# A hybrid decoder kernel on one core: the gated-delta stage goes from units of four heads by 512 tokens to units of eight heads by 256 tokens

## What is computed

```python
q, k, v = silu(causal_conv4(x @ Wq)), silu(causal_conv4(x @ Wk)), silu(causal_conv4(x @ Wv))   # per channel, 4 taps
g = -exp(A_log) * softplus(x @ Wfa @ Wfb + dt_bias);  beta = sigmoid(x @ Wb)
q = l2norm(q) * K**-0.5;  k = l2norm(k)
def step(S, qt, kt, vt, gt, bt):              # S: 128 x 128 per head, one step per token
    S = S * exp(gt)[..., None]
    vd = (vt - einsum('hkv,hk->hv', S, kt)) * bt[..., None]
    S = S + kt[..., None] * vd[:, None, :]
    return S, einsum('hkv,hk->hv', S, qt)
o = o * rsqrt(mean(o*o) + EPS) * o_norm_w * sigmoid(x @ Wga @ Wgb)
out = o @ Wo
```

## Time and profile before

| what | value |
|---|---|
| median of 3 runs | 3720.73 us |
| the profiled execution | 3717.97 us, span 3715.8 us |
| PE busy | 3474.6 us (94%), 37416 instructions |
| DVE, ACT, POOL busy | 1941.4, 1427.4, 125.0 us |
| mean granted TensorE clock | 0.965 |
| delta stage | about 912 to 3020 us of the span |

### The profile page before, as it was taken

The page is one execution under the profiler, slowest core; times in us unless marked ns, Lnnn a source line. Parts: engine busy times, 40 slices in busy tenths (PEclk is TensorE's granted clock), DMA queues, the critical chain, the costliest instruction groups (busy, mean ns, idle before and its releaser), DMA issues. The chain is left out here.

```text
span 3715.8 us, 86134 instructions
## 1 busy us (share of the span) xinstructions
PE 3474.6 (94%) x37416; PEld 1694.5 (46%) x37416; DVE 1941.4 (52%) x3334; ACT 1427.4 (38%) x3313; POOL 125.0 (3%) x457
## 2 busy tenths in 40 slices
PE   6979999996789999999999999999999759999999
PEld 4454444442344544444444444444444435444444
DVE  2131111113778897789878878887888431111111
ACT  1010000001466656666665666566656521000000
POOL 0000000000000000000000000000000000000000
PEclk9979999997989999999999999999999868999999
DMA  4011100003111111121111111111211042000000
GB/s 154 7 57 36 28 0 29 11 0 120 48 31 36 42 50 34 45 66 41 33 56 43 48 50 45 42 37 39 65 39 34 16 154 63 14 15 29 0 12 12
DMA packets 83725, 156.21 MB, mean 42 GB/s; under 512 B 8782, under 2 KB 33998, under 8 KB 79516
## 3 DMA queue, kind: packets, MB, share of 16 engines
q1 hardware_dynamic: 83356, 150.77, 12.3%
HBM read 133.71 MB, written 17.04 MB: 41 GB/s over the span
## 5 line engine op out<-in xcount | busy, mean ns | idle before, releaser
L1333 PE MATMUL psum<-dl_xt,dl_wqkv 128*128 128x512 f32 x1536 | 778.2, 624 | 10.4 <-DVE dl_qkv L977 10.0
L513 DVE SCALAR_TENSOR_TENSOR f_act_g<-psum,f_bup,f_act_g 128x512 f32<-128x512 f32 x96 | 72.1, 751 | 939.4 <-ACT f_act_g L468 939.4
L977 DVE SCALAR_TENSOR_TENSOR dl_qkv<-psum,dl_par,dl_qkv 128x511 f32<-128x511 f32 (+2 forms) x576 | 430.4, 747 | 14.0
L468 ACT ACTIVATE f_act_g<-psum,f_bgate 128x512 f32<-128x512 f32 x96 | 66.0, 687 | 923.1 <-PE psum L411 923.1
L1333 PEld LDWEIGHTS psum<-dl_xt,dl_wqkv 128*128 128x128 f32 x1536 | 257.4, 189 | 250.2 <-issue 212.5
L411 PE MATMUL psum<-xnt_sb,wup 128*128 128x512 f32 x768 | 345.2, 592 | 0.0
L407 PE MATMUL psum<-xnt_sb,wgate 128*128 128x512 f32 x768 | 345.2, 592 | 0.0
L429 PE MATMUL psum<-f_wdown,f_hidden 128*128 128x512 f32 x768 | 344.9, 592 | 0.0
L1340 PE MATMUL psum<-dl_wo,dl_sg 128*128 128x512 f32 x512 | 260.9, 623 | 2.9 <-DVE dl_qkv L977 2.5
L407 PEld LDWEIGHTS psum<-xnt_sb,wgate 128*128 128x128 f32 x768 | 145.9, 190 | 183.7 <-issue 183.7
L411 PEld LDWEIGHTS psum<-xnt_sb,wup 128*128 128x128 f32 x768 | 145.9, 190 | 183.7 <-issue 183.7
(11 more groups left out here) (192 smaller groups left out, 4618.1 us busy)
## 6 DMA issues: line engine op xcount, KB each, us to landing
dl_wqkv<-in_dw_qkv SPq DMA_DIRECT2D x192, 256.0 KB, 2.6
dl_wo<-in_dwo SPq DMA_DIRECT2D x16, 1024.0 KB, 5.2
f_weights_b<-f_weights_by_expert SPq DMA_DIRECT2D x48, 256.0 KB, 6.3
wgate<-in_wgate SPq DMA_DIRECT2D x2, 3072.0 KB, 18.6
wup<-in_wup SPq DMA_DIRECT2D x2, 3072.0 KB, 24.7
f_wdown<-in_wdown SPq DMA_DIRECT2D x2, 3072.0 KB, 13.6
x_sb<-in_x SPq DMA_DIRECT2D x4, 1024.0 KB, 9.3
x_after_experts<-x_sb SPq DMA_DIRECT2D x16, 256.0 KB, 2.0
```

The costliest lines, as they stand in the source:

```text
L977: tap_ = lambda dl: dve.scalar_tensor_tensor(y_[:, dl:TT], ps[:, bank, 0:TT - dl], par[:, h, 4 * a + 3 - dl:4 * a + 4 - dl], y_[:, dl:TT], ...
L1333: last = pe.matmul(ps[:, bank, :], wq[:, n % RING, m, :], xt[:, u // HG % 2, m, :], start=(m == 0), stop=(m == KC - 1))
```

## The change

HU = 8 heads in a unit (two halves HE of HJ = 4), TT = 256 tokens, so again 16 units (2 head groups by 8 token tiles), of 8 slots. The scan's groups hold both halves: 16 instructions each. There are 24 "proj" jobs a unit, each four matmuls 128x259: the tile is loaded with the three tokens before it (HALO), so `boundary`, the tails and L984 go. "rows" is two 128-token tiles a unit, each summed over eight heads in one bank (in four parts q of two matmuls). Long jobs are whole, four a slot: one behind `output_inner`, two behind `solve_u` and the shorts at "inner", one behind `state_step`. All jobs share banks 4 to 7. `krow` and `vrow` use true transposes. GpSimd takes over the series, `near_zero`, `decayed`, the early keys and `o_scale`; level jobs are no longer halved. `choose` and `softplus` are one step behind `add_state` of slot 1. A silu waits for eight convolutions, of 256 tokens; the convolutions of a slot's first two or three long jobs now stand ahead of its `add_state`. The ring for weights is six, `wo` comes in quarters of 512 KB (64 loads), and the output tile is stored every second unit. Cut to its core:

```diff
-HG = 4
+HE = 2
+HU = HJ * HE
+HG = H // HU
-TT = 512
+TT = 256
-RING = 4
+RING = 6
+JOB_BANKS = (4, 5, 6, 7)
...
+def main_jobs(k, sl):
+    if sl in (3, 4):
+        jobs = [("rows", k - 1, i, q) for q in (2 * sl - 6, 2 * sl - 5) for i in range(RB)]
+    else:
+        unit, first = {0: (k + 1, 8), 1: (k + 1, 12), 2: (k + 1, 16), 5: (k + 1, 20), 6: (k + 2, 0), 7: (k + 2, 4)}[sl]
+        jobs = [("proj", unit, first + n, 0) for n in range(4)]
...
+    table = {(0, "long"): [("vrow", k, 1)], (0, "inner"): [("vrow", k, 2)], (0, "split"): [("vrow", k, 3)],
+             (1, "inner"): [("gate", p, 0), ("gate", p, 1)], (1, "split"): [("gate", p, 2)], (1, "end"): [("gate", p, 3)],
+             (2, "inner"): [("turn", p, 0), ("turn", p, 1)], (2, "split"): [("turn", p, 2)], (2, "end"): [("turn", p, 3)],
+             (3, "states"): [("level", w, 0)], (3, "long"): [("level", w, 1)], (3, "end"): [("level", w, 2)],
+             (4, "states"): [("sums", w, 0)], (4, "long"): [("level", w, 3)], (4, "end"): [("level", w, 4)],
+             (5, "long"): [("level", w, 5)],
+             (6, "long"): [("krow", w, 0), ("dec", w2, 0)], (6, "inner"): [("krow", w, 1), ("dec", w2, 1)],
+             (6, "split"): [("dec", w2, 2)], (6, "end"): [("dec", w2, 3)],
+             (7, "states"): [("cross", w, 0)], (7, "long"): [("krow", w, 2)], (7, "inner"): [("krow", w, 3), ("corner", w, 0)],
+             (7, "end"): [("vrow", w, 0)]}
```

GpSimd's order of work for each k, and the series (six operations on 128x2048):

```diff
+                    if prep:
+                        near_zero(w)
+                    if post:
+                        o_scale(p)
+                    if prep:
+                        decayed(w, QQ)
+                        decayed(w, KK)
+                        for lv in range(1, LEVELS + 1):
+                            early_keys(w, lv)
+                        solve(w)
+                    if ahead:
+                        series(w2)
...
+                    for n, c in enumerate((1.0 / 3.0, -0.5, 1.0)):
+                        if n == 0:
+                            pool.tensor_scalar(poly[:, :], all_w, -0.25, c, ALU.mult, ALU.add).then_inc(s["series"], 1)
...
+                        pool.tensor_tensor(poly[:, :], poly[:, :], all_w, ALU.mult).then_inc(s["series"], 1)
```

VectorE in a slot, `by_rows` on TensorE, and TensorE's order in a slot:

```diff
+                        convolutions(done_before, sl)
+                        if sl in (3, 4, 5) and prep:
+                            late_tokens(w, 2 * sl - 5)
                         if run:
                             add_state(k, sl)
...
+                        convolutions(done_behind, sl)
...
-                    for m in range(4):
-                        for j in range(HJ):
-                            last = pe.matmul(ps[part(j), bank, P * m:P * m + P], chunk(src, g0 + m)[:, j, :], ident,
-                                             start=True, stop=True)
+                        last = pe.transpose(ps[:, bank, P * m:P * m + P], src[:, g].rearrange("p j t -> p (j t)"), ident)
...
                         if put_out:
                             output_inner(*previous)
+                        all_main(main[0:1])
                         all_short(k, sl, "long")
                         if run:
                             solve_u(k, sl)
                         all_short(k, sl, "inner")
+                        all_main(main[1:3])
                         if run:
                             state_step(k, sl)
                         all_short(k, sl, "split")
+                        all_main(main[3:4])
                         all_short(k, sl, "end")
```

More of the change, by code:

```diff
@@ L544, in short_jobs @@
 def short_jobs(k, sl, at):
     w, w2, p = k + 1, k + 2, k - 1
[L548 to L562, removed]
@@ L564, in short_jobs @@
+    once = {(1, "end"): ("beta", w, 0), (3, "split"): ("ga", w, 0), (4, "split"): ("fa", w2, 0)}.get((sl, at))
     jobs = [once] if once and once[1] % HG == 0 else []
[L565 to L568, removed]
+    return [j for j in jobs + table.get((sl, at), []) if 0 <= j[1] < UNITS]
 def place_jobs():
-    used, place = [0] * 8, {}
@@ L589, in place_jobs @@
+    last = {job: n for n, job in enumerate(order)}
+    ends, used, place = {b: -1 for b in JOB_BANKS}, {b: 0 for b in JOB_BANKS}, {}
+    for job in order:
+        if job not in place:
+            bank = min(JOB_BANKS, key=lambda b: ends[b])
+            place[job] = (bank, used[bank])
+            used[bank] += 1
+            ends[bank] = last[job]
     return place
@@ L878, in inverse_norms, with shorts, taps @@
                     act.activation(f, f, ACT.Exp, scale=-0.5).then_inc(s["roots"], 1)
+                def shorts(k, sl, at):
+                    for job in short_jobs(k, sl, at):
+                        if job[0] not in ("level", "turn", "sums", "cross", "corner"):
+                            short(job)
+                def taps(jobs):
+                    for job, _ in jobs:
+                        if job[0] == "proj":
+                            tap(*job[1:])
                 for k in range(-2, UNITS + 1):
@@ L942, in _ @@
-                        if job and job[0] == "proj":
-                            tap(*job[1:])
-                        for job, _ in short_jobs(k, sl, "end"):
-                            if job[0] not in ("level", "turn", "sums", "cross", "corner"):
-                                short(job)
-                        if sl == 9 and prep:
-                            inverse_norms(w)
             @block.vector
@@ L1346, in by_rows @@
+                        if q == 3:
+                            last.then_inc(full[bank], 1)
+                        elif i == RB - 1:
+                            last.then_inc(s["wo_read"], 1)
+                def by_rows(bank, src, n):
                     for m in range(4):
[L1347 to L1349 removed]
```

843 lines of the change are left out of this document (407 added, 436 removed).

## The result

The changed kernel takes **4024.4 us** (median of four runs, 4014.1 to 4031.5) against 3720.6 us: 1.082 times as long, 95% interval 1.079 to 1.0845. The forecast was 3640 us, with 3555 to 3730 as its range: the sign is wrong, and the range misses by 294 us. The profiled execution of the changed kernel took 4025.6 us, with a span of 4023.8.

A forecast was written before the change was run, and what follows sets the result against it. TensorE's own instruction sequence was taken as the bound. A unit of 111.0 work plus 8.5 idle is 119.5 us, -70 over 15 steps; with -10 at the ends, 3718.0 becomes 3638, median 3640 us, range 3555 to 3730.

The forecast's parts named there:

- signs of being wrong: Wrong if projections start over 0.24 us apart, POOL takes over 5.5 us, or PE idles over 13 us a unit.
- the ends: Start and end of the kernel: -3 us at the start, -7 from about three slot pairs, -10 in all.
- PE's sum: TensorE's work per unit: scan groups -3.1, `krow` and `vrow` -4.6, edges -2.6, halo +0.8; 111.0 us needed.
- that rival (3790): Short projections pay for their weights, +10 us a unit with idle as forecast: 3790 us, chance 0.02.
- Transfers hidden: Weight loads, `wo` pieces and output stores stay hidden; if not, up to 2 us a unit.
- Where PE will wait: TensorE's idle time per unit, walked slot by slot: waits sum to 11.5 us, taken as 8.5, bounds 3.8 and 13.
- the taps behind the silus: ScalarE's taps stand behind silus: part of waits of about 2 us each in slots 0 and 6.
- banks held by convolutions one slot late: Rival: small waits, such as banks 4 to 7 held, eat the gain; idle 12 to 13, about 3715 us, chance 0.12.
- successive waits share their slack: An engine late in one slot is not later in the next for the same reason: 11.5 us becomes 8.5.
- GpSimd: Operations of 2048 elements at 3.9 us (upper end 7.7), early keys about 2; some 55 us of the unit's 115.
- POOL late: Rival: at 7.7 us an operation, `decayed` ahead of level 1 (slot 3) and `choose` (slot 1) delay: 3850 us, chance 0.15.
- The rival on the slower side: Slower outcome, chance 0.17: late GpSimd results (0.15, 3850 us) plus short projections paying for weights (0.02).

The follow-up runs named there:

- e14: Changed kernel with both `gated` of slot 2 on VectorE moved behind convolution 15, ahead of `add_state`: 3952.6 us, 1.062 times the kernel before.
- e15: Changed kernel with convolution 14 moved ahead of `choose` in slot 1 on VectorE: 3973.9 us, 1.067 times the kernel before.
- e1: Changed kernel with GpSimd's new operations cut to a sixteenth of their width, a probe that leaves out work: 3890.7 us, 1.046 times the kernel before.
- e7: Changed kernel with VectorE's three moves, the series' adds written with two operations, and ScalarE's later taps ahead of silus of q and v: 3803.0 us.
- e9: Changed kernel with GpSimd's new operations at 1/16 width (work left out), VectorE's three moves, and ScalarE's later taps ahead of silus of q and v: 3741.8 us.

## Why the prediction was wrong

Of the prediction's own signs of being wrong one came true: PE idles over 13 us a unit. By its own steps, for the profiled execution (4025.6 against 3638 forecast, 388 us): the unit came out 24.9 us too long (374 us), the ends -13.9 + 19.2 = +5 instead of -10.

- **PE's sum, 111.0 us: right.** 110 at the full clock. Projections start 0.23 us apart (2111.66 to 2113.51 us, eight), 0.01 above what 259 columns cost at 0.84 ns. So a short projection pays for its weights at most that, some 2 us a unit and not 10; that rival (3790) is out. The state step took 0.65 (2110.04 to 2110.69), not 0.86, which gives 1.7 of it back. Four full-width transposes at 2140.31 have the next group 0.53 behind them, as in the earlier trace rows.
- **Transfers hidden: right.** The loads take 2.6 and 3.6 us, and no wait for them stands among PE's costliest.
- **Where PE will wait, 8.5 us, bounds 3.8 to 13: the step that failed.** It is 26.2. The walk followed each engine's order only as far as the scan's own chain and the levels. It found the taps behind the silus (slots 0 and 6; mended, they are worth 31 to 47 us) and the tap behind the decay's Exps (slot 2), but not the two costliest waits, turn 2 on turn 0's bank and the next user of projection 14's bank (gate 3 or projection 16), 122 us by e14 and e15. It had no term either for the gaps without a releaser, 6.0 of the 26.2. The diff says that all jobs share banks 4 to 7; the prediction put "banks held by convolutions one slot late" into a rival of 12 to 13 us idle and 3715 us, without asking for each job which one held its bank before and where that one's reader stands. Also "successive waits share their slack", by which 11.5 became 8.5, is not borne out: taken away together, the causes give back their sum to within 14 us.
- **GpSimd: too small in price, and in the wrong place.** 3.9 us was taken for each of the 2048-element operations; they measure 4.5 for two tensors and 5.4 to 5.5 for the three of one operation, and only those come near the 5.5 of the rival "POOL late". The early keys take 3.38 us in the mean, not 2: 2.0 to 2.9 by themselves, and 4.1 to 5.0 where a VectorE product began before them. Its forecast place (`decayed` ahead of level 1, slot 3) is not where it hurts in steady work: from 1200 to 3100 us no row has PE waiting for L791. Before that, where the first units are prepared, PE waits 14.3 us for `decayed` and the early keys. The rest of its 134 us shows as VectorE's instructions stretched under it and as waits for the comparison. What GpSimd does to VectorE beside it was costed at nothing: VectorE's own times were taken as if GpSimd were idle, as in the earlier trace rows. VectorE is busy 92.6 us a unit, where about 85 was forecast, and 83.8 in e1. The Trainium skill (GPSIMD Engine Reference, 1) says that GpSimd contends with VectorE's instructions that have two SBUF inputs; the trace agrees, 3.72 against 1.26 us for L1099's 1024 elements with and without it. It also shows convolutions and `add_state`, with one input in PSUM, untouched (482 ns in both).
- **The clock: no term.** The sum priced all of PE's work at the full clock of the earlier trace rows. With the idle time the granted clock fell to 0.93 in the window, and 118.2 us of busy time took the place of 110: some 8 us a unit, about 120 us of the 388. With idle 15.5 us (e7) it is 0.96, with 13.6 (e9) 0.97.
- **The rival on the slower side** had GpSimd as its mechanism. That is a third (134 of 384 us); VectorE's and ScalarE's order around the shared banks are 147 to 163, and about 100 stay.

Of the 384 us between forecast and measurement e9 gives back 283 with three edits, one of which leaves work out. The rest is 13.6 instead of 8.5 idle, and 113.2 instead of 111.0 busy, a unit: (5.1 + 2.2) x 15 = 110. The 13.6 are 6.1 of gaps without a releaser and 7.5 of small waits ("level" and "cross" for VectorE, r, dec 0) that were left as they are. So the gaps alone exceed the 5.1 us by which the idle time is over the forecast; their cause stays open.

## What to carry to other kernels

When jobs share a rotation of PSUM banks, list for each job the one that held its bank before and the place of that one's last reader in its engine's queue; a wait there is as real as one in the recurrence, and TensorE pays it twice, in idle time and in clock. Work moved to GpSimd isn't free because GpSimd has room: price each form of operation by itself, and price what VectorE does in that time again. Then test a part at a time: of this change the u product behind a long job pays in the new order and true transposes of v pay in the old one, and the latter alone beats both kernels. And look at the idle time that has no releaser before you promise to remove the rest.

## What was not expected of the hardware

- A GpSimd `tensor_scalar` over 128x2048 float32 takes 5.48 us with one operation (add) in place, 1.90 to 2.02 with two (multiply, add); a comparison takes 5.37 us, and with a multiplication behind it 7.08.
- A VectorE product of two SBUF tensors that starts while GpSimd works on its product L804 ends about its own length behind GpSimd's end. All 16 of L1099's 1024 elements do (1.08 us behind it) and all 29 of L1096's 2048 that so start (2.15 us behind it): they stand until GpSimd is through. Here L804 ends at 2154.17 and L1099 at 2155.25:

```profile
2151.53 3.72 DVE L1099 TENSOR_TENSOR dl_dec<-dl_dec 128x1024 f32<-128x1024 f32 x1
```

```profile
2149.21 4.96 POOL L804 TENSOR_TENSOR dl_qkv<-dl_qkv,dl_dec 128x1024 f32<-128x1024 f32 x1 [9.23 <-PE psum L1440]
```

- The other way round it is the same: GpSimd's product over 128x1024 with one broadcast operand (L804) takes 2.0 to 2.9 us, by level, in 44 of its 80 runs. In the other 36, which start while VectorE works on L1096, it takes 4.1 to 5.0 us and ends 1.9 to 2.7 us behind L1096. The mean is 3.38.
- VectorE instructions of 16 elements take 0.17 to 0.29 us, and now and then up to 3.9 beside a GpSimd operation of over 1 us: 5 of the 36 that overlap one in the changed kernel, none of the 92 others. What tells the five from the rest is not shown.
